# A Mamba block with a mixture of experts on one core: the experts' up products with stationary weights fetched from DRAM for every tile

## The reference, cut to what matters

```python
logits = xf @ gate_w.T
rw, sel = jax.lax.top_k(logits, TOP_K)          # TOP_K = 2, E = 8
rw = jax.nn.softmax(rw, axis=-1)
for e in range(E):
    we = jnp.sum(jnp.where(sel == e, rw, 0.0), axis=-1)
    h = jax.nn.silu(xf @ w1[e].T) * (xf @ w3[e].T)   # 256 -> 512, twice: the up products
    out = out + h @ w2[e].T * we[:, None]            # 512 -> 256: the down product
```

## Time and profile before

| | us |
|---|---|
| median of three runs | 3352.16 |
| profiled execution | 3366.11 |
| its span | 3364.7 |
| state-space, projection and attention stages, to about | 2669 |
| router and routing blocks, to the first transpose of the expert block | 2669 to 2846 |
| expert block, 72 tiles | 2846 to 3274 |
| gather block | 3277 to 3365 |

### The profile page before, as it was taken

The page is one execution under the profiler, slowest core; times in us unless marked ns, Lnnn a source line. Parts: engine busy times, 40 slices in busy tenths (PEclk is TensorE's granted clock), DMA queues, the critical chain, the costliest instruction groups (busy, mean ns, idle before and its releaser), DMA issues. The chain is left out here.

```text
span 3364.7 us, 45342 instructions
## 1 busy us (share of the span) xinstructions
PE 2891.2 (86%) x12880; PEld 1110.5 (33%) x12881; DVE 2419.1 (72%) x2674; ACT 1913.4 (57%) x3514; POOL 1090.7 (32%) x652
## 2 busy tenths in 40 slices
PE   5798889899765849999999999999999772999990
PEld 1234334334332512222222222222222252666650
DVE  0699999999997758888888888888888173111113
ACT  3556655665642417788787878787887611222220
POOL 2889778778862530000000000000000045000006
PEclk8999999999998969999999999999999975999995
DMA  1111111111111532111111111111110145111114
GB/s 42 42 50 48 41 55 56 38 51 49 40 44 43 180 96 39 39 39 39 39 39 39 39 34 37 37 39 39 39 39 10 43 148 188 44 47 44 46 36 147
DMA packets 123093, 185.25 MB, mean 55 GB/s; under 512 B 30224, under 2 KB 77968, under 8 KB 122896
## 3 DMA queue, kind: packets, MB, share of 16 engines
q1 hardware_dynamic: 109072, 142.95, 15.0%
q0 software_dynamic: 13824, 39.86, 3.7%
HBM read 138.01 MB, written 44.43 MB: 54 GB/s over the span
## 5 line engine op out<-in xcount | busy, mean ns | idle before, releaser
L1529 DVE TENSOR_REDUCE nmh<-ring 128x2 f32<-128x1024 f32 x1024 | 1195.9, 1219 | 198.3 <-PE ring L1406 198.1
L1387 ACT ACTIVATE prob<-s_ps 128x512 f32<-128x512 f32 x2048 | 1073.0, 603 | 284.2 <-PE s_ps L1427 284.2
L767 DVE TENSOR_TENSOR_SCAN h<-dA,state,bx 128x512 f32<-128x512 f32 x512 | 618.0, 1263 | 117.3 <-ACT dA L606 117.3
L391 POOL TENSOR_TENSOR bx<-u,bb 128x2048 f32<-128x2048 f32 x128 | 578.8, 4527 | 193.7 <-DVE h L767 193.5
L1427 PE MATMUL s_ps<-qs,ks 98*128 98x512 bf16 x2048 | 614.8, 388 | 17.9 <-issue 12.2
L1439 PE MATMUL acc<-prob,vst 128*32 128x512 f32 x4096 | 550.0, 609 | 0.2 <-ACT prob L1387 0.2
L606 ACT ACTIVATE dA<-dt,aneg 128x512 f32<-128x512 f32 x512 | 348.8, 691 | 270.4 <-DVE h L767 270.3
L673 PE MATMUL y_ps<-h,ident 128*128 128x512 f32 x1024 | 480.4, 613 | 1.1 <-DVE h L774 1.1
L1406 PE MATMUL ring<-k,q 64*128 64x512 bf16 x2048 | 348.6, 395 | 43.6 <-DMA k<-parts 23.9
L1427 PEld LDWEIGHTS s_ps<-qs,ks 98*128 98x128 bf16 x2048 | 149.4, 97 | 582.4 <-ACT prob L1387 474.9
L774 DVE TENSOR_TENSOR h<-h,c_ps 128x2048 f32<-128x2048 f32 x128 | 289.6, 2262 | 4.5 <-PE c_ps L652 4.2
(11 more groups left out here) (221 smaller groups left out, 2562.9 us busy)
## 6 DMA issues: line engine op xcount, KB each, us to landing
bb<-b_rows SPq DMA_DIRECT2D x128, 256.0 KB, 3.2
q<-parts SPq DMA_DIRECT2D x256, 64.0 KB, 2.1
parts<-part POOLq DMA_DIRECT2D x48, 256.0 KB, 3.1
qs<-parts SPq DMA_DIRECT2D x192, 64.0 KB, 2.7
ks<-parts SPq DMA_DIRECT2D x192, 64.0 KB, 2.8
xt<-slots_in POOLq DMA_DIRECT2D x72, 128.0 KB, 2.3
slots_out<-yt SPq DMA_DIRECT2D x72, 128.0 KB, 1.7
k<-parts SPq DMA_DIRECT2D x256, 32.0 KB, 2.0
```

Source lines behind the costliest of these rows:

```text
L391: nc.gpsimd.tensor_tensor(bx[:, n % BR], u[:, b], bb[:, n % RB, None, :].to_broadcast([P, KI, CH]), ALU.mult).then_inc(s_bx, 1)
L767: nc.vector.tensor_tensor_scan(h[:, n % HR, d, :], dA[:, d % 2, :], bx[:, n % BR, d, :], state[:, b, n, d:d + 1], ALU.mult, ALU.add).then_ ...
L1387: nc.scalar.activation(prob[:, k % PR, j, :], s_ps[:, tile % SR, :], ACT.Exp, scale=SC).then_inc(s_exp, 1)
L1529: nc.vector.tensor_reduce(nmh[:, slot, t, 2 * s:2 * s + 2], ring[:, s, :, :], AX.X, ALU.max, negate=True).then_inc(s_free[s], 1)
```

## The change

`w1` and `w3` no longer stand in SBUF; in the router block SP issues 8 loads in place of 24. In the expert block SP reads the tile's expert number and fetches that expert's `w1` and `w3` from DRAM, 512 KB each, into a ring `wu` of four tiles. The up products take pieces of 128 x 128 of them as the stationary operand and 128 token columns of `xT` as the moving one, so that they come out with the inner values on the partitions. The transposes of `mid`, `m_ps` and ACT's copy go away, and DVE writes `midT` itself. The down product follows one tile behind. `g` is freed before the expert block, so POOL waits for the scatters at the end of the routing block.

```diff
-        w1 = sb("w1", [P, NE, KM, FI])
-        w3 = sb("w3", [P, NE, KM, FI])
-        g = sb("g", [P, NT, DM])
...
+            g = sb2("g", [P, NT, DM])
...
-                        for dst, src in ((w1, w1T), (w3, w3T), (w2, w2T)):
+                        for dst, src in ((w2, w2T),):
...
+                pool.wait_ge(s_sc, 16 * (2 * NT + NE))
...
+            WR = 4
-            mid = sb3("mid", [P, 2, FI])
+            wu = sb3("wu", [P, WR, 2, KM, FI])
-            m_ps = ps3("m_ps", [P, KF, P])
...
-                for j in range(NJ - 4, NJ + 2):
+                for j in range(NJ - 4, NJ + 1):
...
+                def weights(j, slot):
+                    e = sp.value_load(expert[0:1, bass.ds(j, 1)], min_val=0, max_val=NE - 1)
+                    wait_apart(sp, s_up, j - WR + 1, s_we)
+                    for k, w in ((0, w1T), (1, w3T)):
+                        sp.dma_start(wu[:, slot, k], w[bass.ds(e, 1)].rearrange("o (k p) n -> p (o k) n", p=P)
+                                     ).then_inc(s_wu[slot], 16)
+
+                for j in range(WR):
+                    weights(j, j)
+                sp.wait_ge(s_we, 16 * NE)
                 with sp.Fori(1, NJ // 4) as n:
                     for q in range(4):
-                        store(4 * n + q, q)
+                        weights(4 * n + q, q)
+                        store(4 * n + q - 4, q)
+                for j in range(NJ - 4, NJ):
+                    store(j, j % 4)
...
-                    if there(j, 1):
-                        wait(act, s_mp, j)
-                        wait(act, s_dn, j - 2)
-                        nc.scalar.copy(midT[:, (q - 1) % 2], m_ps[:, :, :]).then_inc(s_mT, 1)
...
                     if there(j, 0):
                         wait(dve, s_sl, j + 1)
-                        wait(dve, s_mp, j - 1)
-                        nc.vector.tensor_tensor(mid[:, q % 2, :], sl[:, q % 2, :], c_ps[:, q % 2, :], ALU.mult
-                                                ).then_inc(s_mid, 1)
+                        wait(dve, s_dn, j - 1)
+                        nc.vector.tensor_tensor(midT[:, q % 2].rearrange("p k n -> p (k n)"), sl[:, q % 2, :],
+                                                c_ps[:, q % 2, :], ALU.mult).then_inc(s_mid, 1)
...
+                def up(j, q, n):
+                    wait(pe, s_xT, KM * (j + 1))
+                    wait(pe, s_wu[q], 32 * (n + 1))
+                    wait(pe, s_mid, j - 1)
+                    for w, dst in ((0, a_ps), (1, c_ps)):
+                        for m in range(KF):
+                            for k in range(KM):
+                                last = nc.tensor.matmul(dst[:, q % 2, m * P:(m + 1) * P],
+                                                        wu[:, q, w, k, m * P:(m + 1) * P], xT[:, q % 2, k, :],
+                                                        start=(k == 0), stop=(k == KM - 1))
+                    last.then_inc(s_up, 1)
+
+                def down(j, q):
+                    e = pe.value_load(expert[0:1, bass.ds(j, 1)], min_val=0, max_val=NE - 1)
+                    wait(pe, s_mid, j + 1)
+                    wait(pe, s_yt, j - 1)
+                    for m in range(KF):
+                        last = nc.tensor.matmul(o_ps[:, q % 2, 0:DM], midT[:, q % 2, m, :],
+                                                w2[:, bass.ds(e, 1), m, :].rearrange("p o n -> p (o n)"),
+                                                start=(m == 0), stop=(m == KF - 1))
+                    last.then_inc(s_dn, 1)
...
                     if there(j, -1):
                         turn_rows(j + 1, *at(q, n, -1))
...
+                    if there(j, 0):
+                        up(j, q, n)
                     if there(j, 1):
...
+                        down(j - 1, (q - 1) % 4)
```

More of the change, by code:

```diff
@@ L2145, in moe_stage @@
             s_mid = sem("m_mid")
-            s_mp = sem("m_mp")
-            s_mT = sem("m_mT")
+            s_wu = [sem(f"m_wu{r}") for r in range(WR)]
             s_dn = sem("m_dn")
@@ L2193, in store @@
                     sp.dma_start(y_dram[bass.ds(j * P, P), :], yt[:, slot, :]).then_inc(s_y[slot], 16)
-                sp.wait_ge(s_we, 16 * 3 * NE)
-                for j in range(4):
-                    store(j, j)
+                def weights(j, slot):
[7 more added lines that the diff above has]
+                sp.wait_ge(s_we, 16 * NE)
                 with sp.Fori(1, NJ // 4) as n:
                     for q in range(4):
-                        store(4 * n + q, q)
+                        weights(4 * n + q, q)
+                        store(4 * n + q - 4, q)
+                for j in range(NJ - 4, NJ):
+                    store(j, j % 4)
                 for slot in range(4):
@@ L2205, in _, with rows @@
             def _(act):
-                def rows(j, q, n):
+                def rows(j, q):
                     wait(act, s_xp, j + 1)
@@ L2214, in step @@
                     if isinstance(j, int) and j == 0:
-                        rows(0, 0, 0)
+                        rows(0, 0)
                     if there(j, -1):
-                        rows(j + 1, (q + 1) % 4, 0)
-                    if there(j, 1):
-                        wait(act, s_mp, j)
-                        wait(act, s_dn, j - 2)
-                        nc.scalar.copy(midT[:, (q - 1) % 2], m_ps[:, :, :]).then_inc(s_mT, 1)
+                        rows(j + 1, (q + 1) % 4)
                     if there(j, 0):
@@ L2230, in _, with take_y @@
             def _(dve):
+                def take_y(j, q, n):
+                    slot, taken = at(q, n, 2)
+                    wait(dve, s_dn, j - 1)
+                    wait(dve, s_y[slot], 16 * taken)
+                    nc.vector.tensor_copy(yt[:, slot, :], o_ps[:, q % 2, 0:DM]).then_inc(s_yt, 1)
                 def step(j, q, n):
                     if there(j, 2):
[L2233 to L2236, removed]
+                        take_y(j, q, n)
                     if there(j, 0):
                         wait(dve, s_sl, j + 1)
-                        wait(dve, s_mp, j - 1)
-                        nc.vector.tensor_tensor(mid[:, q % 2, :], sl[:, q % 2, :], c_ps[:, q % 2, :], ALU.mult
-                                                ).then_inc(s_mid, 1)
+                        wait(dve, s_dn, j - 1)
+                        nc.vector.tensor_tensor(midT[:, q % 2].rearrange("p k n -> p (k n)"), sl[:, q % 2, :],
+                                                c_ps[:, q % 2, :], ALU.mult).then_inc(s_mid, 1)
                 every_tile(dve, step)
+                take_y(NJ + 1, (NJ + 1) % 4, (NJ + 1) // 4)
             @block.tensor
             def _(pe):
-                pe.wait_ge(s_we, 16 * 3 * NE)
+                pe.wait_ge(s_we, 16 * NE)
                 def turn_rows(j, slot, taken):
@@ L2267, in step @@
                         turn_rows(j + 1, *at(q, n, -1))
[L2268 to L2276, removed]
-                    if there(j, 1):
[L2278 to L2291, removed]
+                    if there(j, 0):
+                        up(j, q, n)
+                    if there(j, 1):
+                        down(j - 1, (q - 1) % 4)
                 every_tile(pe, step)
```

## The result

| | before | changed |
|---|---|---|
| median, five runs each | 3353.70 us | 3333.88 us |
| ratio | | 0.9935 (95% interval 0.9909 to 0.9960) |
| profiled execution's span | 3364.7 us | 3336.6 us |

The change makes the kernel 0.4 to 0.9% faster. The medians lie 19.8 us apart, and 3328 with a range of 3311 to 3348 was forecast. On the chip of the last experiments, medians of 11 and 6 runs were 3364.34 and 3343.32 us, 21.0 apart, with a ratio of 0.9933 (0.9921 to 0.9946).

What follows compares the result with a forecast made beforehand. The prediction took PE's order of work in the expert block as the bound. Its terms, -31.7 + 8.6 + 1.7 - 1.2 - 1.3 = -23.9 us, took the median from 3352.2 to 3328 us, range 3311 to 3348.

Steps and rivals of the forecast that it cites:

- PE's list is the time: Middle of the expert block: PE's order of work sets the time; dropping the transposes of `mid` saves 0.44 us a tile, 31.7 us.
- A load of a full float32 piece hides behind 128 columns: Up products: weight loads lie almost wholly under 128-column matmuls, 0.111 us a pair, between bounds of 0.107 and 0.190.
- The term of +8.6 us: Up products: 32 pairs at 0.111 take 3.55 us, 0.12 more than before, over 72 tiles.
- The first and second rivals: Up products: loads half exposed, 0.150 a pair, about 3418, chance 6%; wholly exposed, 0.190, about 3510, chance 3%.
- The weights cost 0 in the loop: Expert block: fetching 1.31 MB a tile at 238 GB/s is hidden by the four-tile ring, over 14 us for a 6.3 us landing.
- The third rival: Expert block: weights come late and PE waits in every tile, +0.5 us a tile, +35, about 3386; chance 5%.
- The router block gives 0: Router block: 16 fewer weight loads bring nothing, since POOL's issues set when the expert block starts.
- The start: Expert block's start: POOL's moved wait and barrier, about 0.6 us, then the first weights' landing make it +1.7 us.
- my own sign of about 2 us later: Expert block's start: forecast right if the first up product comes about 2 us later than before, counted from the last scatter.
- the upper bound of +5: Expert block's start: worst case of the delay, +5 us, if the four tiles' weight loads share the engines.
- The first tile and the end: Expert block's ends: the 1.19 us wait for the first `mid` goes (-1.2); the end shrinks from 5.5 to 4.2 us (-1.3).
- The sum: Whole kernel: -31.7 + 8.6 + 1.7 - 1.2 - 1.3 = -23.9 us, median from 3352.2 to 3328.

Runs made afterwards that it cites:

- the last experiments: Changed kernel again, without the moved wait, and with first weights issued early, five rounds each on one chip: ratios 0.9933, 0.9934 and 0.9923 to the kernel before.
- 64 column run: Changed kernel with each up matmul cut in two of 64 columns, 64 loads and 64 matmuls a tile: 3615.7 us.
- the early start: Changed kernel with g and the ring kept to the end and the first four tiles' weights issued in the routing block: median 3339.2 us, ratio 0.9923.

## Why the prediction was right

**PE's list is the time.** Right. The transposes' 0.44 us and the up products' price decide, and nothing else changed in the loop.

**A load of a full float32 piece hides behind 128 columns.** Right, and better founded than the forecast could make it. The step took 0.111 us from the 0.110 of a handover and the 0.113 of the 16 logit matmuls; measured were 0.1116. The term of +8.6 us was (3.57 - 3.43) x 72 = +10.1: the pair costs 0.1116 and its columns 0.107, so 128 columns are slightly too few. The loop has runs of 32 such pairs, where I had seen single loads only. The first and second rivals, half or wholly exposed loads, fall with it. The Trainium skill's "TensorE: Matmul & The Clock Gate", section Back-to-back issue gap, gives 81 ns for a pair where the bare matmul needs 56, scaled to float32 as an estimate 0.155 us here; the runs show 0.1116 in float32, at 128 and at 64 columns, and the measurement decides. The same page of the Trainium skill has a section What happens when you issue a matmul, by which loads are pulled ahead of running matmuls into a background buffer. The 64 column run agrees with it: its pairs cost 0.1116 and not 0.1116 + 0.053.

**The weights cost 0 in the loop.** Right, and shown from both sides: the ring can be halved for nothing, and by the estimate above the bytes would have to reach 2.1 MB a tile. The slack was said to be 14 us; with a ring of two, 7.5 us from one use of a slot to the next, no wait appeared in the loop either. The third rival is out.

**The router block gives 0.** Right, although the first profile spoke against it by 8.7 us.

**The start.** Wrong, by my own sign of about 2 us later. The size was half of it and the reason another. I wrote +1.7 for the landing of the weights after the barrier; it was +3.3 to +3.7, and the weights were there in time. The kernel without the moved wait shows that: from its first turn to its first up product it took 1.92 us, as with the early start, whose weights had been issued 20 us before. The moved wait added 1.2, where I had 0.6 from no row, and the first weights, issued before `xt`, delayed `xt` by 2.4 to 2.6. I had them compete only at the upper bound of +5, and among themselves.

**The first tile and the end.** -1.2 and -1.3 were forecast. From the first up product to the end of the last copy it took 424.6 us before (2848.91 to 3273.52) and 399.4 after (2848.36 to 3247.73), 25.2 less, of which 21.6 are the tiles: 3.6 at the two ends. The extra 1.1 is clock: the 1.2 GHz at the block's start covered `a_ps` and most of `c_ps` of tile 0 before, and `a_ps` alone after (2.77 us for `c_ps` became 1.81). That is not the change's doing but luck: in the ring of two, which starts in the same way, `c_ps` of tile 0 took 2.84 again.

**The sum.** -23.9 was forecast for -21.6 in the profiled pair, -22.5 in the second (against the same profile of the kernel before), -19.8 and -21.0 between the medians. The misses are +1.5 for the pairs, +1.6 to +2.0 for the start, and about -1.1 at the ends. That they partly cancel is luck; the tiles alone, -23.1 forecast and -21.6 measured, are not.

## What to carry to other kernels

If a product's result has to be turned for the next product, swap its operands. The turn then costs nothing, as long as each stationary piece is followed by as many columns as its load takes to hide: in float32 here 128 columns were all but enough for a 128 x 128 piece (0.107 us of 0.1116), and 64 cost as much as 128. Before judging a fetch from DRAM, take the bytes of a step over its time, and look at what stands behind the first loads of a block rather than at the loop. A difference in a stage that the change touches only from the side needs a second profile before it gets a cause.

## What was not expected

A small DMA of POOL's, issued 0.6 us behind one pair of 512 KB loads of SP's on an idle core, landed 2.5 us later than alone (first turn 4.9 to 5.3 us after the issue against 2.4 to 2.6), and it made little difference whether one, two or four pairs were in the queue (4.9, 5.0 to 5.1, 5.0 to 5.3). And a wait that leaves PE idle for 3.9 us of 11.5 costs another 2 us in clock: `a_ps` went from 1.78 to 3.25 us.
